# Heads of the last attention's first two batches woven into the causal attention, from its 19th pair on

## What is computed

```
# causal attention (heads of 64), per batch
scores = einsum('biph,biqh->biqp', K, Q)
scores = where(tril(ones((256, 256))), scores, -1e10)
attn = softmax(scores / sqrt(64), axis=-1)
z = einsum('biph,biqp->biqh', V, attn)
out = einsum('bqf,df->bqd', z.reshape(b, 256, 1024), W_O)
x = layernorm(x + out)
# cross attention (heads of 8), per batch
scores = einsum('bhqd,bhkd->bhqk', heads(x @ Wq + bq), heads(ctx @ Wk + bk)) / sqrt(8)
out = einsum('bhqk,bhkd->bhqd', softmax(scores, axis=-1), heads(ctx @ Wv + bv))
x = layernorm(x + concat(out) @ Wo + bo)
```

## Time and profile before

| | us |
|---|---|
| runs of the kernel before | 826.92, 814.76, 813.08 |
| median | 814.76 |
| the profiled execution | 812.73 |
| its span in the profile | 810.9 |
| outside the span | 1.8 |
| PE busy, PE weight loads | 726.4, 537.8 |
| DVE, ACT, POOL busy | 492.8, 413.1, 290.0 |
| mean granted TensorE clock | 0.934 of full |

### The profile page before, as it was taken

How to read it: one execution, slowest core, us unless ns; L and a number is a source line. 1 busy time by engine, 2 the same in 40 slices (tenths; PEclk the granted TensorE clock), 3 DMA queues, 4 the chain that set the end, 5 groups by cost and what they waited for, 6 DMA issues and landing times.

```text
span 810.9 us, 16176 instructions
## 1 busy us (share of the span) xinstructions
PE 726.4 (90%) x5744; PEld 537.8 (66%) x5744; DVE 492.8 (61%) x1309; ACT 413.1 (51%) x1047; POOL 290.0 (36%) x398
## 2 busy tenths in 40 slices
PE   5559898899998999999999989989898899999986
PEld 3336476665756566699888877857576445667665
DVE  3557798877869588254543446545445658674653
ACT  2215357565665576754544448655563544454311
POOL 0013455554556467320000008333331555454300
PEclk9959799999999999899999999999999656899999
DMA  7563343624427374000000000001010520000000
GB/s 238 156 140 74 87 95 78 149 52 110 109 53 190 85 174 159 2 1 1 1 1 1 1 1 4 1 1 36 6 40 5 171 82 26 9 2 8 8 7 7
DMA packets 25174, 48.10 MB, mean 59 GB/s; under 512 B 7264, under 2 KB 14192, under 8 KB 25096
## 3 DMA queue, kind: packets, MB, share of 16 engines
q1 hardware_dynamic: 24376, 45.66, 21.9%
q10 hardware_dynamic: 720, 1.41, 0.5%
HBM read 17.49 MB, written 0.52 MB: 22 GB/s over the span
## 4 chain that ended last, share of the span: by engine, by line
PE 62%; DVE 15%; issue 10%; ACT 7%; POOL 3%; DMA 2%; SPq 1%; POOLq 0%; DVEq 0%; ACTq 0%
PE G L522 8%; PE SC L772 7%; PE SC L759 7%; PE SC L702 5%; PE G L563 4%; PE SO L745 3%; DVE shift_cols L1471 3%; PE SC L794 3%; PE G L871 3%; ACT causal_probs L1085 2%; PE SO L826 2%; PE SC L678 2%; PE G L527 2%; PE SM L719 2%; PE G L585 2%
## 5 line engine op out<-in xcount | busy, mean ns | idle before, releaser
L1100 ACT ACTIVATE exps<-SC 128x512 f32<-128x512 f32 x192 | 114.2, 596 | 112.6 <-PE SC L702 112.0
L1471 DVE TENSOR_REDUCE shift_cols<-SC 128x2 f32<-128x512 f32 x192 | 129.7, 683 | 35.5 <-PE SC L678 34.6
L1550 POOL TENSOR_TENSOR rstd<-variance,consts 128x2 f32<-128x2 f32 (+1 forms) x48 | 37.2, 775 | 286.6 <-DVE variance L1164 283.7
L1619 POOL TENSOR_TENSOR VB<-exps 128x256 f32<-128x256 f32 x128 | 95.0, 749 | 65.1 <-ACT exps L1100 64.4
L1074 ACT ACTIVATE hidden<-SC,cols 128x256 f32<-128x256 f32 x128 | 53.5, 470 | 66.3 <-PE SC L759 66.1
L1641 POOL TENSOR_TENSOR causal_probs<-causal_probs,inverse 128x256 f32<-128x256 f32 x64 | 51.6, 828 | 70.5 <-DVE inverse L1484 70.5
L1505 DVE SCALAR_TENSOR_TENSOR R<-SC,small,R 128x128 f32<-128x128 f32 x128 | 39.0, 346 | 55.6 <-PE SC L772 55.0
L1085 ACT ACTIVATE causal_probs<-SC,negmax 128x128 f32<-128x128 f32 (+1 forms) x128 | 52.2, 423 | 37.2 <-DVE negmax L1479 37.0
L702 PE MATMUL SC<-stacked_q,stacked_k 100*128 100x256 f32 x256 | 66.5, 343 | 4.5 <-DMA stacked_q<-shift_rows 3.0
L772 PEld LDWEIGHTS SC<-ffn_w,hidden 128*128 128x128 f32 x512 | 66.0, 192 | 5.3 <-issue 1.8
L678 PE MATMUL SC<-stacked_k,stacked_q 96*128 96x256 f32 x256 | 56.6, 308 | 12.7 <-DVE shift_cols L1471 7.4
(11 more groups left out here) (244 smaller groups left out, 1500.1 us busy)
## 6 DMA issues: line engine op xcount, KB each, us to landing
stacked_k<-k_hi SPq DMA_DIRECT2D x64, 128.0 KB, 2.3
stacked_q<-q_hi SPq DMA_DIRECT2D x64, 128.0 KB, 2.4
ffn_w<-in_ffn_w SPq DMA_DIRECT2D x16, 512.0 KB, 4.6
stacked_k<-k_lo SPq DMA_DIRECT2D x32, 128.0 KB, 2.4
stacked_q<-q_lo SPq DMA_DIRECT2D x32, 128.0 KB, 2.4
packed_k<-U SPq DMA_DIRECT2D x48, 32.0 KB, 1.9
packed_q<-YN SPq DMA_DIRECT2D x48, 32.0 KB, 1.9
a_weights<-in_a_li SPq DMA_DIRECT2D x3, 256.0 KB, 8.2
```

Source lines behind the costliest of these rows:

```text
L1100: fn(exps[:, n % EXPS, :, :].rearrange("p t q -> p (t q)"), SC[1][:, n % 2, :, :].rearrange("p t q -> p (t q)"), ACT.Exp, scale=ATTENTIONS ...
L1471: v.tensor_reduce(shift_cols[:, n // UNIT % 4, :, n % UNIT], SC[0][:, n % 2, :, :], axis=AX.X, op=ALU.max, negate=True).then_inc(head_max, 1)
L1619: v.tensor_tensor(kept[n % EXPS].rearrange("p t q -> p (t q)"), exps[:, n % EXPS, 0, :], exps[:, n % EXPS, 1, :], ALU.add).then_inc(kept_r ...
```

## The change

The two attentions overlap. Pairs 0 to 18 stand in the slots where they stood (203 to 221); from the 19th pair (number 18) on the pairs stand in every second slot: 221, 222, 224, 226 and so on to 246. `LX_AT` becomes 221, so heads 128 to 155 (all 16 of batch 0 and 12 of batch 1) stand one in each of the slots 221 to 248, and head 156 in slot 249 is the first without a pair beside its scores. All that hangs on `LX_AT` (`cross_values`, `mix`, `LAST`) moves up by 14 slots; the program has 14 slots fewer. No arithmetic is added or removed; two small `memset` are new, and the load of ACT's exponential table stands at the start of the causal attention and no longer at its end.

PSUM is shared out again for the slots of the weave: the pairs from 18 on use the tile SC0 alone, the scores of the woven heads one bank of SC1, their transposed products its other bank. So pair i waits for the exponentials of pair i-1 (before: i-2), a woven head's scores for the maximum of the head just before it, its transposed product for the exponential of the head before it. The pairs' values and the heads' values share one ring on SO. The heads' values move from `VB` to new buffers `VX`, the key sums to the space of weights that are used up, the outputs of batches 0 and 1 to `HE`. `causal_in(3)` is spread over 11 slots (before: 8), `causal_out(b)` makes both its projections in one slot, 3 slots before `cross_in(b)`. The loads of the second mixture's experts stand behind the last pair's values.

```diff
-LX_AT = L1_AT + NB * PAIRS
...
+ALONE = 18
+LX_AT = L1_AT + ALONE
+WOVEN_END = STACK_HEADS + 2 * (NB * PAIRS - ALONE)
...
+def pair_slot(i):
+    return L1_AT + (i if i <= ALONE else 2 * i - ALONE - 1)
+
...
+def pair_of(slot):
+
+    return PAIR_AT.get(slot)
...
+def pair_values_slot(u):
+    i = 2 * u + 1
+    return pair_slot(i) + LAG + (2 if i < ALONE else 3)
+
+
+PAIR_AT = {pair_slot(i): i for i in range(NB * PAIRS)}
+VALUES_OF = {pair_values_slot(u): u for u in range(NB * PAIRS // 2)}
...
 def causal_in_at(b):
-    return settle_at(b) + 5 if b < 2 else L1_AT + PAIRS * (b - 1) + 1
...
+def causal_in_steps(b):
+
+    return ((0, 1, 2, 3), (6, 7)) if b < 2 else ((0, 2, 4, 6), (3, 5)) if b == 2 else ((0, 2, 6, 10), (4, 8))
+
...
 def causal_out_at(b):
-    return L1_AT + PAIRS * b + 13
+    return pair_values_slot(4 * b + 3) + 1
...
 def cross_in_at(b):
-    return L1_AT + PAIRS * b + 18 if b < 2 else LX_AT + HEADS * (b - 2) + 12
+    return causal_out_at(b) + 3
...
         VB = [sb(f"VB{k}", [P, 2048]) for k in range(2)]
+        VX = [sb(f"VX{k}", [P, TT * C + HD - HD0]) for k in range(2)]
...
+        added = [W[n][:, T * k:T * k + T] for n in ("a2_wq", "a2_li1", "a2_li2", "a2_li3") for k in range(2)]
+
+        def key_sum(n):
+            return kept[n % EXPS].rearrange("p t q -> p (t q)") if n < STACK_HEADS else added[n % EXPS]
...
+        outputs_of = [OB[:, 0:4, :], OB[:, 4:8, :], carve(HE, 0, 4, T), carve(HE, 1024, 4, T)]
+
+        def outputs(s):
+
+            return outputs_of[s % 2 + (2 if s in (LX * NB, LX * NB + 1) else 0)]
...
-        RINGS = {"g": [g[:, :] for g in G], "unit": [SM[:, :]], "out": [SO[:, 0:T]], "up": sc[0:2],
-                 "down": sc[2:4], "pair": [SO[:, :]]}
+        RINGS = {"g": [g[:, :] for g in G], "unit": [SM[:, :]], "out": [SO[:, :]], "up": sc[0:2],
+                 "down": sc[2:4]}
...
+        def score_bank(n):
+            return SC[1][:, 0, :, :] if STACK_HEADS <= n < WOVEN_END else SC[0][:, n % 2, :, :]
+
+        def turned_bank(n):
+            return SC[1][:, 1 if STACK_HEADS <= n < WOVEN_END else n % 2, :, :]
...
+        def pair_bank(i):
+            return SC[i % 2 if i < ALONE else 0]
+
+        def causal_place(b):
+            return min(b, 1)
...
                     for t in range(TT):
-                        yield t
                         project_out(L1 * NB + b, t)
-                    yield 4
+                    yield 2
                     normal_transposed(b, 7, X[b])
...
                     if n == STACK_HEADS:
+                        pe.wait_ge(exp_ready, ALONE)
+                    elif STACK_HEADS < n < WOVEN_END:
+                        pe.wait_ge(head_max, n)
+                    elif n == WOVEN_END:
                         pe.wait_ge(exp_ready, NB * PAIRS)
-                    if n >= 2:
+                    elif n >= 2:
                         pe.wait_ge(head_max, n - 1)
...
                     for t in range(TT):
-                        last = mm(SC[0][:, n % 2, t, :], q[:, t * P:(t + 1) * P], kk, start=True, stop=True)
+                        last = mm(score_bank(n)[:, t, :], q[:, t * P:(t + 1) * P], kk, start=True, stop=True)
                     last.then_inc(shift_scores, 1)
...
-                    if n >= 2:
+                    if STACK_HEADS < n < WOVEN_END:
+                        pe.wait_ge(head_exp, n)
+                    elif n >= 2:
                         pe.wait_ge(head_exp, n - 1)
+                    if n == WOVEN_END:
+                        pe.wait_ge(head_max, WOVEN_END)
...
                     for t in range(TT):
-                        last = mm(SC[1][:, n % 2, t, :], kk[:, t * P:(t + 1) * P], q, start=True, stop=True)
+                        last = mm(turned_bank(n)[:, t, :], kk[:, t * P:(t + 1) * P], q, start=True, stop=True)
                     last.then_inc(head_scores, 1)
...
                     if n == STACK_HEADS:
-                        wait_emptied(pe, ("OC", 4 * NB - 1))
+                        pe.wait_ge(pads_made, 2)
                     g = fill(pe, "out", ("O", U_))
...
-                    if i >= 2:
+                    if c % 2 == 0:
+                        for side in ("k", "q"):
+                            wait_emptied(pe, (side, L1 * NB + b, c // 2))
+                    if i > ALONE:
+                        pe.wait_ge(exp_ready, i)
+                    elif i >= 2:
                         pe.wait_ge(exp_ready, i - 1)
-                    s = SC[i % 2]
+                    s = pair_bank(i)
...
-                    if u == 0:
-                        wait_emptied(pe, ("O", STACK_HEADS // UNIT - 1))
-                    g = fill(pe, "pair", ("OC", u))
+                    g = fill(pe, "out", ("OC", u))
...
-                    if 0 <= slot - L1_AT < NB * PAIRS:
-                        pair_scores(slot - L1_AT)
+                    if pair_of(slot) is not None:
+                        pair_scores(pair_of(slot))
...
-                    i = slot - L1_AT - LAG
-                    if 0 <= i < NB * PAIRS:
-                        transpose_probs(i)
-                    if 3 <= i < NB * PAIRS + 2 and i % 2 == 1:
-                        pair_values(i // 2 - 1)
+                    if pair_of(slot - LAG) is not None:
+                        transpose_probs(pair_of(slot - LAG))
+                    if slot in VALUES_OF:
+                        pair_values(VALUES_OF[slot])
...
-                    if slot == LX_AT:
+                    if slot == L1_AT:
                         nc.scalar.preload_act_table_set(EXP_AND_LN)
...
                     wait_filled(pool, ("O" if stream_of(n - EXPS) // NB == A1 else "S", (n - EXPS) // UNIT))
-                    if n == STACK_HEADS:
-                        wait_filled(pool, ("OC", 4 * NB - 1))
-                    v.tensor_tensor(kept[n % EXPS].rearrange("p t q -> p (t q)"), exps[:, n % EXPS, 0, :],
+                    v.tensor_tensor(key_sum(n), exps[:, n % EXPS, 0, :],
                                     exps[:, n % EXPS, 1, :], ALU.add).then_inc(kept_ready, 1)
...
-                        yield 1 + u if b < 2 else 2 + 4 * u
...
-                        if slot == LX_AT + 8 + 4 * g:
+                        if slot == pair_values_slot(NB * PAIRS // 2 - 1) + 1 + 2 * g:
```

118 lines of the change are left out of this document (59 added, 59 removed).

## The result

The changed kernel takes 822.33 us (median of 4 runs, 817.66 to 827.08) against 813.92 us for the kernel before (median of 4, 811.91 to 826.92): a ratio of 1.0125, 95% interval [1.0085, 1.0166]. It is slower by 8 to 10 us, within the 2% that count as no change; the forecast was 806 us, range 792 to 821. The profiled execution took 823.05 us, with a span of 821.2.

A forecast was written before the change was run, and what follows sets the result against it. PE bounds the causal attention near full clock; in the cross attention it is busy because its clock is low. Profiled 812.7 us, minus 12.9 between the marks, plus 6.4 given back behind them, made 806 us, range 792 to 821.

The forecast's parts named there:

- the second stretch: Slots 230 to 248 of the weave: nine pairs 55.8 us, slot 248 1.3, `causal_out(2)` 2.7, together 59.8 us.
- the loop of 6.2 us: Two woven slots from slot 230 on: chain from one pair's scores to the next through a head's exponential, 6.2 us.
- Rival B: The weave runs at half clock: its second stretch takes 28 us over 59.8, kernel 834 us; chance 0.08.
- the marks: Maxima of pair 18 and of head 156: 110.1 us apart before, 97.2 forecast, a gain of 12.9 us.
- the first stretch: Slots 221 to 229 of the weave, bound by PE: 33.0 us of work plus waits of 2 and 2.4, 37.4 us.
- the packed operands: Head 128, first of the weave, waits for its operands' DMAs: 2 us, bounds 0 and 4.
- A single product set of a head: PE price of one head's scores, and as much for a transposed product: 0.22 us, from 0.43 for two heads.
- PE's total of 47.4 us: PE's work in slots 230 to 248, summed from full-clock prices: 47.4 us.
- Given back behind the weave: The causal tail now stands beside heads 156 to 164: 6.4 us of exposed PE work, bounds 2 and 12.
- rival A: The clock stays up behind the weave, heads 156 to 164: 10 us come back, kernel 796 us; chance 0.22.
- Rivals C and D: C: queues lock in the weave, loops 7.7 us, 820, chance 0.18; D: head 128 waits for the pairs, chance within C's.

The follow-up runs named there:

- tall_heads: Changed kernel with the cross attention's scores and transposed products over all 128 rows and a tiny exponential scale (wrong result): 813.47 us, ratio 0.9972.
- fill_low: Changed kernel with six added products of 32 rows behind the pair's scores in 13 woven slots, results unused: 872.15 us (853.96 to 882.59).
- tall_lone: no_weave with the heads' scores and transposed products over all 128 rows and a tiny exponential scale (wrong result): 807.41 us, ratio 0.9920.
- first_head_last: Changed kernel with head 128's scores and maximum moved to the end of its slot, behind pair 18: 824.98 us (816.45 to 832.64).
- the second profile: The changed kernel once more, unedited: 823.47 us, ratio 1.0121 to the kernel before.
- tall_scores: no_weave with only the heads' scores over 128 rows, transposed products over 32 as before, and a tiny exponential scale (wrong result): 835.73 us, ratio 1.028.
- lone_light: no_weave with one added f32 product of 128 rows ahead of every second head's scores, 4th to 40th head, results unused: 837.17 us, ratio 1.0269.
- lone_light16: no_weave with four added bf16 products of 128 rows by 128 columns ahead of each head's scores, results unused: 854.07 us, ratio 1.0474.
- no_weave: Changed kernel with its buffers and side steps but no woven slot, all 32 pairs in slots of their own: 815.46 us, ratio 1.0021.

## Why the prediction was wrong

**The step that failed** is the second stretch, "59.8": the loop of 6.2 us was priced at full clock, and the stretch ran at 0.82. The loops themselves were right in kind and nearly in size: 5.95 us in four of tall_heads' nine, and 63.0 for the whole stretch at 0.97. The missing 3.2 us are made of the loop with `causal_out(2)`, 10.2 instead of 8.9, one with unit values, 7.5, two of 6.8 and the last, 7.9 instead of 7.5, less 0.25 in each of the four short ones. The other 12 to 15.5 are the clock.

**Rival B** had this mechanism, at 0.08: "From about a quarter of this stretch at half clock on" the gain is gone, and 27 of 74.8 and 38 of 78.5 us were. What I set against it, that more than half of PE's work there is the pairs', was no reason: with low products of the heads the clock came down beside the pairs' as it did in the heads alone. B's picture of why, PE idle in every loop, holds in part only. By the rule of the Trainium skill ("TensorE: Matmul & The Clock Gate", section "A second HAM failure mode: psum-queue depth-cycling") PE's idle gaps between the banks would do it. In these runs the clock does fall with the longest of them, 2.4 to 2.8 us, but it is 0.97 with 10.9 us of gaps in 62.9 (tall_heads) and 0.66 with 2.1 in 111.6 (fill_low), so gaps alone do not explain this kernel. B's price of 834 is that of the whole stretch at half clock, and 36 and 48% of it were. Per us at half clock B had 0.32 us (28 of 88); between tall_heads and the two profiles it was 0.50 (11.9 for 24 us more of it) and 0.45 (15.5 for 34), so that price was low, not high.

**The comparison was lopsided.** The forecast set a weave at full clock against a stretch that was at half clock for 29 of its 110 us. Of the 12.9 us between the marks, 3.8 were this clock (110.1 before, 106.3 in tall_lone) and 3.7 the weave (102.6); the rest, 5.4, was never there: 2.2 in the first stretch (39.6 in tall_heads for 37.4) and 3.2 in the second.

**Ahead of pair 18** the sum had nothing; 4.6 us were lost (4.5 again). The wait for pair 17's bank, 2.81 us, is nowhere in my sum: I had thought of the packed operands alone, and their 2 us do not show. first_head_last gives 2 us net for it. Of the rest 0.4 are head 128's scores themselves (542.71 to 543.10), and 0.9 are pair 18's at half clock, 2.06 us instead of 1.14 (550.32 to 551.46). The new layout has 0.4 (65.2 in tall_lone, without half clock, for 64.8).

**A single product set of a head** was priced at 0.22 us, from a row of four that take 0.43. That row shows two heads' products running at once. Standing alone, as in the weave, one takes 0.43. Up to four such sets a loop hide in PE's idle time, so the loops came out right in spite of it, but PE's total of 47.4 us was too low: 52.05 in tall_heads. In the first stretch, which PE bounds, nothing hides them: nine sets at 0.21 us more are 1.9 of the 2.2 to 2.6 us that it is longer than forecast.

**Given back behind the weave:** 6.4 in the sum, 2.8 and 1.3 measured, the second below the lower bound of 2. Like against like it is 5.5 (tall_heads to tall_lone). The difference is rival A on a small scale: from head 156 to head 164 the changed kernel has no half clock, where the kernel before had 15.6 us of it, and so it does the causal tail there for 1.2 us more, 20.6 against 19.4, but it is not faster.

**Rivals C and D:** the loops with `causal_out` and unit values do reach 7.5 us and more at full clock, but by their own work. PE's waits in the second stretch (sum in us, number, longest) are for a head's exponential, only once for an emptied bank of any weight, and once, 0.6 us, for an operand (`OB`):

```profile
PE SC L767 <- ACT exps L1163: 8.8, 6, 2.7
...
PE SM L871 <- ACT unit_inverse L1157: 0.6, 1, 0.6
```

D is out: head 128 ran where the diff puts it.

**The sum with measured terms.** Against the forecast's 806.2, in this profile: -7.0 before pair 0, +4.6 to pair 18, +2.6 and +15.0 in the weave, -3.6 behind it, +5.2 to the end, 823.0 (823.05 measured). In the second profile, by spans, with 804.4 forecast: -3.9, +4.5, +2.7, +18.7, -5.1, +0.1, 821.4 (821.3 measured). The terms before pair 0 and behind head 191 lie outside the change and differ between two profiles of the same kernel, that is, they are drift; that of the second stretch is not. In the first profile the two drift terms, -7.0 and +5.2, nearly cancel by luck.

## What to carry to other kernels

Before pricing a rearrangement at one clock, ask what holds that clock in each of its stretches: weaving low products (31 and 32 rows here) between tall ones spread the half clock over the tall ones instead of curing it, and a wait of PE of over 2 us cost more than itself, because half clock followed. Compare like with like: had I priced the old order at full clock too, weaving would have been worth 3.7 us between the marks, less than the bank hand-over (4.0) and the work given back (5.5) cost. And a duration read from a row of several instructions is that of several together; ask whether they overlap before dividing.

## What was not expected of the hardware

- PE's share of busy time did not tell the clock, and the rows of its products counted: 1.00 with six added products of 128 rows a loop, 0.66 with as many of 32 rows, 0.97 and 0.82 for the same 480 products with the heads' over 128 or over 31 and 32 rows. This is no rule of shares: with one kind of the two tall the heads were at half clock for longer than with none.
- Half clock followed PE's longest waits, with tall products too, and lasted longer with low ones: behind a wait of 2.5 to 2.7 us 3.4 us in tall_heads, 6.8 and 10.2 in the changed kernel.
- Being busy did not bring PE back to full clock in tall_scores: 58 us on end at 0.50, in the 44 us shown busy for all of them.
- Products on different rows run at the same time, four in 0.72 us at half clock; beside a product of 128 rows they do not, 1.32 us. The Trainium skill tells of the first ("TensorE: Matmul & The Clock Gate", section "Part 3: Packing small matmuls — row/col tiling"), and the trace agrees; had I read the row of four by it, the 0.22 would not have stood.
- Small doses of tall work did not help at all (lone_light 837.17 us, lone_light16 854.07, no_weave 815.46).
